# A six-sublayer decoder on one core: another order of work in the causal rounds

## The reference, cut to what matters

```
q = einsum('qdh,bcd->bhcq', Q, x) * sq      # 16 heads of 64
k = einsum('qdh,bcd->bhcq', K, x) * sq
v = einsum('vdh,bcd->bhcv', V, x) * sv
att = einsum('bhcq,bhCq->bhcC', q, k) / d_query
att = where(causal, att, -inf)
p = softmax(att, axis=-1)
y = einsum('bhcC,bhCv->bhcv', p, v)
z = einsum('dvh,bhcv->bcd', W, y) * (sqrt(d_embed / d_value) / num_heads)
x = layernorm(x + z)
```

## Time and profile before

| | us |
|---|---|
| median of 3 runs | 2038.26 (2038.09 to 2040.28) |
| the profiled execution | 2034.35 |
| its span, first to last instruction | 2032.5 |
| span outside the instructions (2034.35 - 2032.5) | 1.85 |
| TensorE busy | 1737.9 |
| VectorE busy | 1376.5 |
| ScalarE busy | 1017.1 |
| GpSimd busy | 451.3 |
| causal rounds, first scores to last YT copy | 757.10 to 1419.04 |

### The profile page before, as it was taken

The page is one execution under the profiler, slowest core; times in us unless marked ns, Lnnn a source line. Parts: engine busy times, 40 slices in busy tenths (PEclk is TensorE's granted clock), DMA queues, the critical chain, the costliest instruction groups (busy, mean ns, idle before and its releaser), DMA issues.

```text
span 2032.5 us, 34786 instructions
## 1 busy us (share of the span) xinstructions
PE 1737.9 (86%) x12889; PEld 1263.2 (62%) x12889; DVE 1376.5 (68%) x4874; ACT 1017.1 (50%) x2615; POOL 451.3 (22%) x493
## 2 busy tenths in 40 slices
PE   3678888888788789999999999998879999989808
PEld 1356666666643456676667676666659898974307
DVE  7888888886236966666675566666546667653685
ACT  5545556555257525555553455554125545433752
POOL 4000000000000323333333233333113332320003
PEclk8779888889899979999999999999989999998959
DMA  5000000000002010000000000000323433400001
GB/s 159 1 1 1 1 1 1 1 1 2 1 1 42 21 68 1 1 1 1 1 2 1 1 1 1 1 1 17 122 56 70 95 85 74 95 1 0 0 0 42
DMA packets 86078, 49.56 MB, mean 24 GB/s; under 512 B 40223, under 2 KB 83669, under 8 KB 85717
## 3 DMA queue, kind: packets, MB, share of 16 engines
q1 hardware_dynamic: 80195, 47.18, 9.0%
q10 hardware_dynamic: 5714, 0.16, 0.2%
HBM read 45.24 MB, written 2.10 MB: 23 GB/s over the span
## 4 chain that ended last, share of the span: by engine, by line
PE 56%; DVE 29%; ACT 9%; issue 3%; POOL 2%; POOLq 0%; DVEq 0%; ACTq 0%
PE PS L1739 7%; PE PS L2049 6%; DVE nx L764 6%; DVE sq L773 6%; PE PS L1751 5%; PE PS L1764 4%; PE PS L1725 3%; ACT px L1801 3%; PE PS L2467 3%; DVE cm L1859 3%; PE PS L2112 3%; PE PS L1779 2%; PE PS L2068 2%; DVE PS L1861 2%; PE PS L2077 2%
## 5 line engine op out<-in xcount | busy, mean ns | idle before, releaser
L1905 POOL TENSOR_SCALAR px<-px,crl 128x640 f32<-128x640 f32 (+7 forms) x128 | 226.7, 1781 | 404.2 <-DVE crl L1874 404.2
L1801 ACT ACTIVATE px<-PS,cnm 128x896 f32<-128x896 f32 (+7 forms) x256 | 187.6, 737 | 250.2 <-DVE cnm L1861 248.6
L773 DVE TENSOR_SCALAR sq<-nx 128x4 f32<-128x4 f32 x1024 | 175.1, 171 | 31.4
L764 DVE TENSOR_TENSOR_SCAN nx<-sq 128x6 f32<-128x6 f32 x1024 | 173.8, 170 | 32.0 <-POOL sq L903 0.9
L1859 DVE TENSOR_REDUCE cm<-PS 128x1 f32<-128x512 f32 (+3 forms) x224 | 154.2, 688 | 58.9 <-PE PS L1739 58.9
L1751 PE MATMUL PS<-ident,px 128*128 128x128 f32 x1152 | 155.3, 280 | 34.1 <-ACT qT L1791 20.5
L1751 PEld LDWEIGHTS PS<-ident,px 128*128 128x128 f32 x1152 | 128.6, 141 | 76.5 <-ACT qT L1791 25.5
L2139 ACT ACTIVATE YT<-YT,xnm 128x154 f32<-128x154 f32 x256 | 104.8, 413 | 92.8 <-DVE xnm L2181 92.8
L198 POOL TENSOR_SCALAR rstd<-mv 128x1 f32<-128x1 f32 x80 | 34.1, 426 | 526.1 <-DVE mv L176 526.0
L1739 PE MATMUL PS<-kT,qT 64*128 64x512 f32 (+3 forms) x768 | 147.6, 511 | 0.0
L1764 PEld LDWEIGHTS PS<-pT,V 128*64 128x64 f32 x2304 | 124.3, 137 | 34.4 <-issue 31.5
(11 more groups left out here) (339 smaller groups left out, 3834.5 us busy)
## 6 DMA issues: line engine op xcount, KB each, us to landing
xbs<-in_fside_Bx16xSxS SPq DMA_DIRECT2D x8, 1232.0 KB, 6.5
fsrc<-in_fside_Bx16xSxS SPq DMA_DIRECT2D x8, 1232.0 KB, 6.6
xmk<-in_mask_Bx16xSxS_bk SPq DMA_DIRECT2D x8, 308.0 KB, 8.3
fsrc<-in_mask_Bx16xSxS_bk SPq DMA_DIRECT2D x8, 308.0 KB, 8.4
X<-in_x SPq DMA_DIRECT2D x4, 512.0 KB, 6.8
w<-in_L_attn_W_ffn SPq DMA_DIRECT2D x2, 1024.0 KB, 12.6
t<-in_L_ffn_w SPq DMA_DIRECT2D x2, 1024.0 KB, 11.9
out<-xs SPq DMA_DIRECT2D x16, 128.0 KB, 1.7
```

What stands on the lines that cost most here:

```text
L764: e.tensor_tensor_scan(k.nx[:, t % 2, :], d0, d1, 0.0, ALU.mult, ALU.add).then_inc(sem("rec.scan"), 1)
L773: e.tensor_scalar(place(c % 2 * 2 * W6 + 6 * n + 7), state, 10.0, -10.0, ALU.min, ALU.max).then_inc(sem("rec.clip"), 1)
L1801: e.activation(k.px[n % 2][:, h, c0:c1], row[:, c0:c1], ACT.Exp, scale=-1.0, bias=k.cnm[:, h, slot:slot + 1], accum_out=k.cl[:, h, slot:sl ...
L1905: e.tensor_scalar(x, x, k.crl[:, 0, slot:slot + 1], None, ALU.mult).then_inc(sem("c.normal0"), 1)
```

## The change

The list of a round becomes: `cs(n)`, `beside[n]`, `ce(n,0)`, `cp(n-2)`, `cn(n,0)`, `ct(n-1)`, `ce(n,1)`, `cy(n-2)`, `ctl(n-1)`, `cn(n,1)`. ScalarE's part of `cs` is now the step `ce(n, h)`, one per head. Its part of `ct` copies groups 0 and 1; group 3 is the new step `ctl`; group 2 is always VectorE's (before, every third group went to VectorE in turn). ScalarE's copy to `YT` is the step `cy`. On the first batch's outputs, a pair of `zout` stands in each of the rounds 38 to 41, where before round 38 had four and 39 and 40 two each.

```diff
@@ causal_order
-        chain, n = list(norm_chain(5, T)), ahead + max(i // 2 - 1, 0)
-        beside[n] += ([("zout", T)] if i > 1 else []) + chain[:3]
+        chain, n = list(norm_chain(5, T)), ahead + i // 2
+        beside[n] += [("zout", T)] + chain[:3]
...
-        o.add(("cs", n))
-        if n == ahead:
-            o.add(*[("zout", T) for T in OUTPUTS[:2]])
+        o.add(("cs", n), *beside[n], ("ce", n, 0))
         if n >= 2:
             o.add(("cp", n - 2))
-        o.add(("cn", n, 0), *beside[n])
+        o.add(("cn", n, 0))
         if n >= 1:
             o.add(("ct", n - 1))
+        o.add(("ce", n, 1))
+        if n >= 2:
+            o.add(("cy", n - 2))
+        if n >= 1:
+            o.add(("ctl", n - 1))
         o.add(("cn", n, 1))
     n = len(rounds) - 1
-    o.add(("ct", n), ("cp", n - 1), ("cp", n))
+    o.add(("ct", n), ("ctl", n), ("cp", n - 1), ("cy", n - 1), ("cp", n), ("cy", n))
...
-                by = min(sum(made) % 3, 1)
+                by = int(i != 2)
@@ causal_scalar
+    def ce(n, h):
+        if n >= 2 and h == 0:
+            w.wait_ge("c.turn", k.piece["ct", n - 2, len(causal_groups(n - 2)) - 1][2])
+        row = PS[:, 2 * h:2 * h + 2, :].rearrange("p b q -> p (b q)")
+        w.wait_ge("c.max", rounds.passed(n, len(rounds.tiles[n]) - 1, h))
...
     def ct(n):
+        for i in range(2):
+            turned(n, i)
+
+    def ctl(n):
+        turned(n, 3)
```

More of the change, by code:

```diff
@@ L1791, in cq, with turned, cy @@
         e.mul(k.qT[u % 2][:, blk * 512:(blk + 1) * 512], PS[:, k.room["cq", u, blk][0], :], -1.0 / 256).then_inc(sem("c.q"), 1)
-    def cs(n):
-        if n >= 2:
+    def ce(n, h):
+        if n >= 2 and h == 0:
             w.wait_ge("c.turn", k.piece["ct", n - 2, len(causal_groups(n - 2)) - 1][2])
[L1796 to L1802, removed]
-    def ct(n):
[L1805 to L1811, removed]
+        row = PS[:, 2 * h:2 * h + 2, :].rearrange("p b q -> p (b q)")
+        w.wait_ge("c.max", rounds.passed(n, len(rounds.tiles[n]) - 1, h))
+        for t, u, qt, start in rounds.places(n):
+            c0, c1, slot = start * P, (start + qt + 1) * P, rounds.slot(n, t)
+            e.activation(k.px[n % 2][:, h, c0:c1], row[:, c0:c1], ACT.Exp, scale=-1.0, bias=k.cnm[:, h, slot:slot + 1],
+                         accum_out=k.cl[:, h, slot:slot + 1]).then_inc(sem("c.exp"), 1)
+    def ct(n):
+        for i in range(2):
+            turned(n, i)
+    def ctl(n):
+        turned(n, 3)
+    def turned(n, i):
+        group, (_, _, m) = causal_groups(n)[i], k.piece["ct", n, i]
+        w.wait_ge("c.turn", m)
+        e.copy(k.pT[n % 2][:, 4 * i:4 * i + len(group), :].rearrange("p b q -> p (b q)"), PS[:, k.room["ct", n, i][0], 0:len(group) * P]).then_inc(sem("c.pT.scalar"), 1)
+    def cy(n):
         tiles = rounds.tiles[n]
@@ L1822, in cp @@
         e.copy(dst, PS[:, 6, 0:2 * P].rearrange("p (t q) -> p t q", q=P)).then_inc(sem("c.y"), 1)
-    return {"cq": cq, "cs": cs, "ct": ct, "cp": cp}
+    return {"cq": cq, "ce": ce, "ct": ct, "ctl": ctl, "cy": cy}
 def causal_vector(e, w, k):
@@ L1863, in ct @@
     def ct(n):
[L1864 to L1868, removed]
+        group, (_, _, m) = causal_groups(n)[2], k.piece["ct", n, 2]
+        w.wait_ge("c.turn", m)
+        e.tensor_copy(k.pT[n % 2][:, 8:8 + len(group), :].rearrange("p b q -> p (b q)"), PS[:, k.room["ct", n, 2][0], 0:len(group) * P]).then_inc(sem("c.pT.vector"), 1)
     def cn(n, h):
```

## The result

The changed kernel takes 2060.67 us (median of 4 runs, 2058.75 to 2064.17), the kernel before on the same chip 2039.27 (2038.09 to 2044.05): a ratio of 1.010, 95% interval 1.0088 to 1.0113. It is 21.4 us slower. I had said 2048, 10 us slower: direction and mechanism came as described, at twice the price.

A forecast was written before the change was run, and what follows sets the result against it. TensorE bounds the causal rounds; only its idle time can be won. From the profiled 2034.35 us: - 28.6 + 45.1 - 2.5 - 4.0 = + 10.0, so 2044.4; median 3.9 higher, so 2048, own range 2038 to 2060, wider range 2030 to 2064.

The forecast's parts named there:

- what goes: 66 rounds from round 2: TensorE's waits at transposes for the query eviction and pT vanish, 28.6 us less.
- h1's scores wait: At the scores: h1 waits for its exponentials behind two copies, 0.45 to 0.87 us by tile, all lost.
- the size of that wait: h1's wait at the scores: 0.68 us per round, 45.1 us in 66 rounds.
- the reason why h0 covers nothing: At the scores: matmuls stay in program order, so everything behind h1's waiting first matmul waits as well.
- rival B: At the scores: h0's scores cover 0.43 us of h1's wait, 0.25 per round is left; 2020 us, 6%.
- the ends of the stage: Start and end of the stage: 2.5 us gained up to round 2, net 4.0 gained from round 68 on.
- The rounds without projections: Rounds 68 to 70: 7.3 to 7.5 us each, 22.1 for the three, 4.7 gained.
- the last round of all: Last round: the copies delay the scaling of h1, which nothing covers, by 0.7 us.
- A: At the scores: the wait on h1's exponentials is hidden, only the gains are left, - 35 us, 2003; 8%.
- C: Middle rounds: even exchange, h1's wait 0.5 us rather than 0.68, and waits of their own lost; 2037, 10%.
- D: VectorE becomes the bound, h1's scaling beside GpSimd's, or the clock falls; + 20 us, 2068; 12%.

The follow-up runs named there:

- the one with the heads apart: Changed kernel with the loops over heads and banks exchanged, so all of a tile's h0 stands ahead of its h1: 2061.42 us, ratio 1.010.

## Why the prediction was right or wrong

**Right: what goes.** 28.3 us against 28.6, or against 29.3 with the 0.7 that I had booked at the start for round 2's scores, which lie in these rounds; nine rounds without waits take 74.3 against 73.9. The query's eviction is hidden, and both waits of the earlier trace rows left the list. With the choice of groups alone, and projection and eviction where they were, the wait for the eviction stays (17.1 us); with the product put ahead, a new one comes up.

**Right: that h1's scores wait, how the wait grows with the tile, and that it is paid in full.** Forecast 0.56, 0.66, 0.76, 0.87 and 0.45; measured 0.68, 0.79, 0.90, 1.00 and 0.58. The steps between the tiles are right within 0.01, and one, two and three copies move the time by the 0.49 per copy that two copies in 1.08 stand for.

**Wrong: the size of that wait, and this is the term that failed.** I had 0.68 us per round, and it is 0.82 (53.9 over 66 rounds). Each of the five values is 0.12 to 0.14 too small, which is 8.8 of the 11.5 us that were missing. Three small things add up in the same direction. I had TensorE at the scores 1.97 us behind the first transpose and rounded it to 2.0: 0.03. It is there after 1.92 (1016.72 - 14.80): 0.05. And I had the copies begin at 0.64; they begin at 0.70 (1015.50 - 14.80): 0.06. With 1.92 and 0.70 the same sum gives 0.70 for the tile (4,2), where 0.68 or 0.69 was measured. The last two are no misreadings of the kernel before. Of its 22 rounds from 3 to 67 whose transposes run without a pause, 19 have 1.97 and 0.64 to 0.66, and only one (round 43) has 1.92 and 0.69; in the changed kernel all 65 rounds have 1.92 and 0.69 to 0.70. Why both moved is not settled. The wait was a difference of two numbers of about 2 and 2.6 us, taken 66 times: 0.1 us in either is 7 us in the sum. My own range said that (0.15 per round is 10 us), and the value in its middle took both ends as unchanged.

**Wrong in part: the reason why h0 covers nothing.** I leaned on program order. The Trainium skill, "TensorE: Matmul & The Clock Gate", says too that matmuls stay in program order (Part 2, Step-by-step). Here the trace disagrees: with h0's second chunk ahead in the program h1's first still starts 0.95 us before it (1006.76 and 1007.71). What I drew from it for this change, that everything behind the waiting matmul waits as well, does hold (1029.34), but it is not what costs the time. The conclusion held because each head needs its 1.91 us anyway. For rival B that is the end from a better side: neither order of h0's work covered any of it.

**Wrong: the ends of the stage,** 2.5 us together. I counted these rounds up to the start of h1's scores in the next one, and so h1's wait once too often. From h1's start in round 1 to h1's start in round 2 it took 7.78 us (779.30 - 771.52), where I had 7.7; but the round ends at h0's start, after 6.99 (778.51 - 771.52) instead of the 9.49 of before. That this is just my 2.5 us is luck: 0.7 of those belonged to round 2. Against it, h1's start in round 1 came 8.13 us behind round 0 (771.52 - 763.39) instead of 6.68. The 1.45 are the eviction and the table load of 1.28 behind it, which I had not looked for; with both out of the way only 0.09 of them are left. The rounds without projections took 6.68, 6.97 and 6.90 us, where I had said 7.3 to 7.5, together 20.55 rather than 22.1: up to h1's start the first took 7.37. A part of this gain is the clock, 0.87 over these rounds before and 1.00 now, for which I had no term. But the last round of all took 17.43 rather than 15.0. TensorE's timeline there, which answers to the earlier trace rows:

```profile
1434.14 1.99 PE L1754 MATMUL PS<-ident,px 128*128 128x128 f32 x16
1438.56 2.51 PE L1754 MATMUL PS<-ident,px 128*128 128x128 f32 x16 [2.43 <-DVE px L1885]
1441.00 3.01 PE L1767 MATMUL PS<-pT,V 128*64 128x128 f32 x32
```

It waits 2.43 us for VectorE's scaling of h1, which comes last, and then transposes and product take 2.51 and 3.01 instead of 1.99 and 1.97, at a lower clock, as the window of these 8.4 us shows:

```profile
1438.50:1446.86 8.36, 7.42 (x80) 6.62 (x80) 0.69 (x1) 2.29 (x5) 0.00 (x0) 0.80 0.01 2
```

The version with the eviction behind h0's exponentials has the same order here, kept its clock and took 15.84: so of the 3.2 us, 1.6 are the order's, where I had 0.7, and 1.6 the clock's.

**The rivals.** A and B fell with h1's wait, C with its size. D fell too: the clock is 1.00, and VectorE's scaling takes 0.75 to 0.93 us in rounds 27 to 36 where I expected 1.2 to 1.5, since GpSimd is hardly at work then. It does end late, in round 28 10.7 us behind that round's scores (1027.41 - 1016.72), later than D had it, but this is hidden: in rounds 3 to 67 ScalarE, done with h0's exponentials, always idles 0.4 us or more before the first copy.

## What to carry to other kernels

An engine's copies that wait for the bottleneck's last step must not stand ahead of what the bottleneck's next step waits for. Here no copy between the exponentials, the first group on VectorE and the eviction behind h0's exponentials are together 52 us faster than the change; one copy fewer alone is 36. A wait that is the difference of two chains and is paid in each of 66 rounds has to be known at both ends to 0.02 us, and the change itself may shift them: 0.05 and 0.06 here, which nearly all rounds of the kernel before would have hidden. A wait that one term has must not be counted by another as well. And read a gap from start to start: two halves of the array that work in turn look like a busy engine.

## What the runs showed of the hardware

- Matmuls on different halves of the array's rows run in an order of their own: h1's chunk started 0.95 us before h0's next, which stood ahead of it, and exchanging the loops left the time as it was (ratio 1.000, 604.77 and 604.74 us). Behind a matmul that waits for a semaphore the other half is held too: h0's second chunk started 1.18 us behind its first instead of 0.96, together with h1's.
- The table load of ScalarE (1.28 us) runs when the sequencer comes to it: ahead of a wait it costs nothing (754.23, with the exponential at 761.61), behind a late eviction the full 1.28 (767.96, exponential at 769.25, the maxima there since 767.37).
- After a wait of 2.43 us TensorE's next 8.4 us ran at a mean granted clock of 0.80, and a product took 3.01 us instead of 1.97. Four kernels have this order and this wait (2.43 or 2.44 us): in the changed kernel and the one with the heads apart the clock fell to 0.79 or 0.80, in the one with the product first and the one with the eviction behind it stayed at 1.00. Why is not settled.
